# One transformer layer with FP4 rounding on one NeuronCore: calls reordered one by one, deeper ring buffers, other PSUM banks

## The reference

```python
q = rope(x @ Wq); k = rope(x @ Wk); v = x @ Wv                    # 8 heads, 16 and 32 wide
o = (q * 16 ** -0.5 @ k.T * decay) @ v                            # decay is causal, per head
o = o * rsqrt(mean(o * o) + EPS) * g_norm_w                       # per head
x = layernorm(x + (o * silu(x @ Wg)) @ Wo)
h = silu(fp4(x) @ fp4(w_gate).T) * (fp4(x) @ fp4(w_up).T)         # 352 wide
x = layernorm(x + fp4(h) @ fp4(w_down).T)
```

## Time and profile before

| what | value |
|---|---|
| device time, median of 3 runs | 137.76 us (137.73 to 137.95) |
| span of the profiled execution, first to last instruction | 135.8 us |
| what the median has beyond that span | 1.96 us |
| TensorE matmul busy | 121.6 us, 1248 rows |
| VectorE busy | 112.9 us, 391 rows |
| ScalarE busy | 98.0 us, 311 rows |
| GpSimd busy | 96.6 us, 139 rows |
| chain that ended last | TensorE 75%, VectorE 11%, ScalarE 8% |

### The profile page before, as it was taken

How to read it: one execution, slowest core, us unless ns; L and a number is a source line. 1 busy time by engine, 2 the same in 40 slices (tenths; PEclk the granted TensorE clock), 3 DMA queues, 4 the chain that set the end, 5 groups by cost and what they waited for, 6 DMA issues and landing times.

```text
span 135.8 us, 3550 instructions
## 1 busy us (share of the span) xinstructions
PE 121.6 (90%) x1248; PEld 79.6 (59%) x1248; DVE 112.9 (83%) x391; ACT 98.0 (72%) x311; POOL 96.6 (71%) x139
## 2 busy tenths in 40 slices
PE   4997998999999999999999999999999958888660
PEld 4755574755656566575758584848484745445450
DVE  1269889876879899999999999999999899999710
ACT  3055665778858787787888888888888978876753
POOL 4212856878677778878787979797979697656561
PEclk9999999999999999999999999999999999999999
DMA  3899980000000000000000000000000000000011
GB/s 105 262 250 237 409 288 5 7 2 0 5 0 0 5 0 2 0 7 0 0 5 0 0 7 19 0 19 7 19 0 24 0 19 19 22 19 19 27 54 59
DMA packets 6897, 6.53 MB, mean 48 GB/s; under 512 B 864, under 2 KB 6112, under 8 KB 6752
## 3 DMA queue, kind: packets, MB, share of 16 engines
q1 hardware_dynamic: 5856, 5.56, 13.6%
q10 hardware_dynamic: 1024, 0.76, 1.7%
HBM read 5.26 MB, written 1.05 MB: 46 GB/s over the span
## 4 chain that ended last, share of the span: by engine, by line
PE 75%; DVE 11%; ACT 8%; issue 3%; POOL 2%; POOLq 1%; DVEq 0%; ACTq 0%
PE ps L338 12%; PE ps L357 7%; PE ps L485 6%; PE ps L469 6%; PE ps L462 5%; PE ps L397 5%; PE ps L329 4%; PE ps L387 4%; PE ps L476 3%; PE ps L370 3%; PE ps L405 3%; PE ps L422 2%; PE ps L421 2%; PE ps L413 2%; PE ps L323 2%
## 5 line engine op out<-in xcount | busy, mean ns | idle before, releaser
L902 POOL TENSOR_TENSOR rstd_h<-ms,minus_half 128x8 f32<-128x8 f32 x16 | 26.4, 1647 | 7.7 <-DVE ms L767 7.0
L893 POOL TENSOR_TENSOR qk<-rope_c,rope_s 128x256 f32<-128x256 f32 x16 | 11.6, 726 | 13.0 <-DVE rope_s L744 12.9
L338 PE MATMUL ps<-w_vg,xT_sb 128*128 128x512 f32 x32 | 18.0, 645 | 0.0
L485 PE MATMUL ps<-wd_T,hT 128*128 128x128 f32 x96 | 13.6, 278 | 2.7 <-ACT hT L515 2.7
L927 POOL TENSOR_TENSOR hq<-h_grid,hs 128x352 f32<-128x352 f32 x16 | 13.0, 812 | 3.0 <-DVE h_grid L680 3.0
L516 ACT ACTIVATE q_eo<-ps,consts 128x128 f32<-128x128 f32 x32 | 11.8, 369 | 3.4 <-PE ps L347 3.4
L485 PEld LDWEIGHTS ps<-wd_T,hT 128*128 128x128 f32 x96 | 12.1, 193 | 3.5 <-DVE r L794 2.6
L740 DVE TENSOR_TENSOR rope_c<-ps,tabs_sb 128x256 f32<-128x256 f32 x16 | 6.8, 425 | 8.8 <-PE ps L329 8.8
L515 ACT ACTIVATE raw<-ps 128x512 f32<-128x512 f32 x16 | 9.6, 599 | 5.9 <-PE ps L357 5.9
L897 POOL TENSOR_SCALAR_AFFINE_SELECT probs<-raw 128x512 f32<-128x512 f32 x16 | 10.3, 642 | 4.7 <-ACT raw L515 4.6
L469 PE MATMUL ps<-wgu_T,xqT 128*128 128x352 f32 x32 | 12.4, 469 | 0.2
(11 more groups left out here) (112 smaller groups left out, 363.1 us busy)
## 6 DMA issues: line engine op xcount, KB each, us to landing
tabs_sb<-rope_tables SPq DMA_DIRECT2D x1, 1024.0 KB, 10.8
out<-x SPq DMA_DIRECT2D x16, 64.0 KB, 1.5
tabs_sb<-rope_tables SPq DMA_DIRECT2D x1, 640.0 KB, 7.3
xT_sb<-x_transposed SPq DMA_DIRECT2D x1, 512.0 KB, 8.7
x_res<-x SPq DMA_DIRECT2D x1, 512.0 KB, 11.4
xT_sb<-x_transposed SPq DMA_DIRECT2D x1, 320.0 KB, 6.2
x_res<-x SPq DMA_DIRECT2D x1, 320.0 KB, 7.9
w_vg<-in_w_vg ACTq DMA_DIRECT2D x1, 256.0 KB, 3.4
```

What stands on the lines that cost most here:

```text
L338: mm(vg_ps, xT(c), w_vg[:], start=True, stop=True).then_inc(vg_pe, 1)
L485: last = mm(down_ps, hT[:, c % 2, t, :], wd_T[:, t, :], start=t == 0, stop=t == 2)
L893: gp.tensor_tensor(qk[:, c % D, :], rope_c[:, c % D, :], rope_s[:, c % D, :], ALU.add).then_inc(qk_p, 1)
L902: gp.tensor_tensor(rstd_h[:, c, :], ms[:, c, :], minus_half[:], ALU.pow).then_inc(rms_p, 1)
```

## The change

- The four loops over stages are gone. Each engine's calls are written out one by one with their chunk, in an order that has no period: TensorE 244 calls, ScalarE 292, VectorE 380, GpSimd 128. `rotate` is split into three calls (`rope_cos`, `rope_sin_even`, `rope_sin_odd`), `copy_v_and_silu` into two, each with its place and, on ScalarE, its semaphore; so are the three copies of qkT.
- Rings: `D` is 4 and holds for nearly all buffers, six slots for r1, x_ratio and h_ratio, eight for r2, four for the state. `x_plus`, `x_grid`, `h_plus` and `h_grid` are gone; the steps write x_ratio and h_ratio in place. A few waits for a chunk four back guard v_sb, silu_g, qk and hq.
- PSUM: a table of banks, and one function `occupy` that waits for the readers of what is in the bank. Scores 0 to 3; attention output 4 and 5; transpose_o 2; transpose_y 0; qk, qkT and xqT bank 7; vg, out projection and up bank 6; gate 3; hT 5; down 1; state product 4.
- Three groups of four warm-up matmuls in place of five.

```diff
+    D = 4
...
-        r1 = sb("r1", 128, NC, H)
-
-        r2 = sb("r2", 128, NC, H + 1)
-        r_sq = sb("r_sq", 128, 2, H + 1)
+        r1 = sb("r1", 128, 6, H)
+
+        r2 = sb("r2", 128, 8, H + 1)
+        r_sq = sb("r_sq", 128, D, H + 1)
...
-        x_ratio = sb("x_ratio", 128, 2, H)
-        x_magic = sb("x_magic", 128, 2, H, dt=bf16)
-        x_plus = sb("x_plus", 128, 2, H)
-        x_grid = sb("x_grid", 128, 2, H)
+        x_ratio = sb("x_ratio", 128, 6, H)
+        x_magic = sb("x_magic", 128, D, H, dt=bf16)
...
+        BANKS = {"scV": (0, 1), "scA": (2, 3), "oT": (4, 5), "o": (2,), "yT": (0,), "qk": (7,),
+                 "qkT": (7,), "vg": (6,), "att": (6,), "xqT": (7,), "gate": (3,), "hT": (5,),
+                 "up": (6,), "down": (1,), "U": (4,)}
...
+            def free(n):
+                name = tile.get(n)
+                if name == "scV":
+                    pe.wait_ge(mask_v, filled[name])
...
+                elif name == "o":
+                    pe.wait_ge(gate_v, filled[name])
...
+            def occupy(name, banks):
+                for n in banks:
+                    free(n)
+                    tile[n] = name
                 filled[name] += 1
...
             def project_qk(c):
                 pe.wait_ge(d_wqk, 16)
                 pe.wait_ge(d_x[group(c)], 16)
-                free_qk_bank()
+                occupy("qk", BANKS["qk"])
                 mm(qk_ps, xT(c), w_qk[:], start=True, stop=True).then_inc(qk_pe, 1)
-                fill(4, "qk")
-                if c == 0:
-                    warm_up(4)
...
+            warm_up(4); project_qk(0); warm_up(4); project_vg(0); transpose_qk(0); warm_up(4); state_product(0)
+            project_vg(1); project_qk(1); scores(0); project_vg(2); project_qk(2); from_state(0); values(0)
+            transpose_qk(1); transpose_o(0); state_product(1); project_vg(3); scores(1); from_state(1)
...
+            def copy_v(c):
+                if c >= D:
+                    act.wait_ge(o_pe, c - D + 1)
+                if c >= D:
+                    act.wait_ge(U_pe, c - D + 1)
                 act.wait_ge(vg_pe, c + 1)
-                copy(v_sb[:, c % D, :], vg_ps[:, 0:VD])
-                nc.scalar.activation(silu_g[:, c % D, :], vg_ps[:, VD:2 * VD], ACT.Silu).then_inc(vg_act, 1)
+                copy(v_sb[:, c % D, :], vg_ps[:, 0:VD]).then_inc(v_act, 1)
...
+            def x_plus_(c): quant_plus(x_ratio[:, c % 6, :], x_magic[:, c % D, :], x_ratio[:, c % 6, :], xmagic_a, xquant_v, c)
+            def x_grid_(c): quant_grid(x_magic[:, c % D, :], x_ratio[:, c % 6, :], x_ratio[:, c % 6, :], xquant_v, c)
...
             def rotate_add(c):
+                if c >= D:
+                    pool.wait_ge(qkT_pe, c - D + 1)
+                if c >= D:
+                    pool.wait_ge(U_pe, c - D + 1)
                 pool.wait_ge(rope_v, 3 * (c + 1))
```

633 lines of the change are left out of this document (320 added, 313 removed).

## The result

| | before | after |
|---|---|---|
| median of 4 runs each, taken on the same chip | 137.85 us (137.73 to 138.2) | 142.31 us (140.69 to 142.74) |
| ratio, 95% interval | | 1.0301 (1.0253 to 1.0349) |
| span of the profiled execution | 135.8 us | 140.8 us |

The change makes the kernel 3% slower, and the prediction of 132.9 us was wrong. In the experiments, a run at a lower granted clock that took over 1.5% longer than the kernel's best is left out of the ratio: one each of e6, e10 and e11, three of the four of e8.

What follows compares the result with a forecast made beforehand. It took TensorE to bound the kernel up to out_projection(4), then VectorE: 1.9 + 38.3 + 4.5 + 0.5 + 78.9 + 6.8 = 130.9 us of span, plus 1.96 for 132.9 us. The range was 129.0 to 138.2 us.

Steps and rivals of the forecast that it cites:

- Sum 78.9 us: VectorE's work left after out_projection(4), sixteen quantiser and norm rounds plus remaining attention: 78.9 us, bounds 77 and 82.
- The last 6.8 us as before: From the end of h_grid_(15) through the last calls to the store: 6.8 us, unchanged from the old kernel.
- The head: TensorE up to out_projection(4): 38.3 us of work, 4.5 lost (bounds 3.5 and 7), 0.5 for form changes.
- the predicted wait of `scores(1)` for `gated(0)`: In the head, TensorE waits some 1.4 us because bank 2 is held until VectorE's gated(0) has read it.
- `project_vg(0)`, put down with 1 us: At the start, project_vg(0) falls among TensorE's slow matmuls and costs about 1 us more.
- The changes of matmul form: TensorE switches between narrow and wide matmuls 96 times instead of 79; costs 0.5 us, bounds 0 and 2.
- Deeper rings and in-place steps at nothing: Deeper buffer rings and writing x_ratio and h_ratio in place add no instruction and cost nothing.
- (c): Slower: after out_projection(4), TensorE and VectorE wait for each other on PSUM bank 7; 138.1 to 142 us, chance 0.13.
- (b): Handover waits on in-order queues, in the head and at bank 7, eat 3 to 5 us; 135.5 to 137.5, chance 0.12.
- (a): Both engines do a little better: VectorE keeps the end phase's pace, head wait covered; 129 to 131 us, chance 0.22.
- The signs I listed for "wrong": VectorE idle over 3 us behind 45 us, TensorE at out_projection(4) later than 47 us, or an end over 7.5 us.
- the sign for "right": VectorE nearly without idle time from about 45 us to the last h_grid_, at 124 us in place of 128.98.

Runs made afterwards that it cites:

- e6: The changed kernel with 56 unread matmuls put between TensorE's last calls; 150.15 us, ratio 1.0886 to the kernel before.
- e10: The changed kernel with VectorE's and GpSimd's calls reordered (284 and 77 instructions moved) so the two seldom meet; 142.18 us, ratio 1.0275 to the kernel before.
- e11: The kernel of e10 with the eight unread TensorE matmuls of e9 near the end; 142.05 us, ratio 1.0293 to the kernel before.
- e8: The changed kernel with only VectorE's and GpSimd's calls reordered so the two seldom meet, an earlier order than e10; 142.88 us, too few runs for a ratio.
- e1: The changed kernel with GpSimd's five wide operations made narrow from chunk 4 on, part of the result left out; 135.16 us, ratio 0.9808 to the kernel before.
- e9: The changed kernel with eight unread matmuls in TensorE's pauses near the end; 141.15 us, ratio 1.0235 to the kernel before.
- e3: The changed kernel with the plus step of x and h written to another buffer instead of in place; 142.19 us, ratio 1.0301 to the kernel before.
- e4: The kernel before, its order and PSUM banks kept, with the change's deeper rings and in-place steps; 137.77 us, ratio 0.9996 to the kernel before.
- e5: A separate program running three kinds of VectorE step alone and beside GpSimd operations; the two-SBUF-input step took 0.45 us alone, 1.03 beside products.

## Why the prediction was wrong

- **The step that failed: "Sum 78.9 us" for VectorE's work that is left.** It counted instructions and took their durations from the old kernel's end phase. Those durations are not the instructions' own: they hold in an order in which these steps don't meet GpSimd's. The round that was read there, from 108.47 on, has no meeting. VectorE took 86.04 us, 0.65 of it waiting. With GpSimd's wide operations made narrow the same instructions took 79.84 (e1). So 6.2 of the 7.1 us missing are the meetings, shown; the count itself was 0.9 too low. The step asked of each engine how full it is and who waits for whom; it never asked what two engines do to each other while neither waits. GpSimd, 71% busy in the old kernel, did not occur beside VectorE in the sum.
- **Why the order decides it.** With a period, each stage has the same neighbours. In the old order one step of the sixteen in a round meets something, in eight of the stages, at 0.11 us each, 0.9 in all. Without a period each of the 96 quantiser steps has its own neighbour; 26 of them were held up, by 0.31 us on average.
- **"The last 6.8 us as before"** was 8.56, with a granted clock of 0.52 in it. e9 gives 6.87 at a clock of 1.0, so the work was counted rightly. The clock was not foreseen. The old kernel's TensorE is hardly busier at that point (6.55 us of the 9.0 before its last `h_grid_`, against 6.63 of 9.24) and kept its clock. Its pauses there are shorter, 0.67 us against up to 0.87, but e3 kept its clock with the longer ones; why the one does and the other mostly doesn't was not settled.
- **The head** was about right in its sum, in part by luck. `out_projection(4)` ends at 46.2 against 45.2. TensorE worked 42.4 us of it (forecast 38.3 + 2.6 + 0.5 = 41.4) and paused 1.9 (1.4 + 0.5). But these are three pauses: `transpose_qk` waits 0.78 us for rope, which must read bank 7 first, and `values` 0.59 for GpSimd's mask, where I had found no other wait over 0.2 up to out_projection(1) and 0.5 for the rest; the predicted wait of `scores(1)` for `gated(0)` is there, at 0.54 us in place of 1.4:

```profile
16.25 0.71 PE L344 MATMUL ps<-q_eo,kT 32*128 32x256 f32 x8 [0.54 <-DVE gate_o L780]
```

And `project_vg(0)`, put down with 1 us as one of the slow calls, was not slow in this execution (1.04 us) but was in e1 (1.86), whose head ends 0.8 us later for it.

- **The changes of matmul form** cost nothing behind the changeover, as forecast: VectorE never waits for TensorE there. In the head they are not separated: TensorE worked 1.0 us more than the sum had, and part of that may be theirs.
- **Deeper rings and in-place steps at nothing**: right, by e3 and e4.
- **The rivals.** (c) gave 138.1 to 142, which all but holds the result, by a mechanism that did not occur: VectorE never waited for bank 7 behind the changeover and was busy for all of 43.53 us. A right number there is no merit. (b) did not occur either, as TensorE's pauses in the head add up to what the sum had for them, and (a) is out of reach even without the meetings: e1 is at 135.2. The signs I listed for "wrong" were idle time and late or long stretches; the length of equal instructions was not among them. None of them came up except the long end, and that by the clock and not by the calls of ln2 and the stores that I had named; the sign for "right", VectorE without pauses, did, and only the place of the last `h_grid_`, 132.24 in place of 124, told that something was off.

The Trainium skill names this contention ("SBUF — State Buffer", sections "SBUF: two separate sides" and "Who interferes with whom"): VectorE and GpSimd share a pair of ports, a VectorE instruction with two SBUF inputs and a GpSimd operation that reads SBUF exclude each other, and whichever starts first blocks the other. I had not weighed this rule in the prediction. The traces agree on who collides (e5: 1.03 us in place of 0.45; the PSUM and one-input steps untouched) and that the start decides (0.03 us behind a `y` a step keeps its length, 0.05 behind it doesn't). They differ in two things: GpSimd's powers on 8 columns read SBUF and held up nothing, and a blocked step ends as if released about 0.13 us before the end of GpSimd's operation as recorded, not at it (0.37 to 0.38 us behind it, with 0.51 us of work).

## What to carry to other kernels

Before a reordering, list for the bounding engine which of its instructions share something with a neighbour engine's, and take their length in the new order from that, not from their mean in the old one. An engine that shows no idle time may still lose time; compare the mean of equal instructions between two profiles, and look at the few that are far over the median together with what runs beside them. A periodic order with few such meetings is worth keeping: here it had eight small ones in its stages, and none of the aperiodic orders tried had fewer than twelve, up to 0.64 us each.
